# Where GpSimd splits the last four batches of keys, and the bias additions, in a gated two-layer kernel

## What is computed

```python
x = x + tanh(g_xattn[0]) * L0_xattn(ctx_1024, layernorm(x))   # dynamic time warping
x = x + tanh(g_ffn[0])   * L0_ffn(layernorm(x), w1, conv_w, conv_b, w2)
x = x + tanh(g_xattn[1]) * L1_xattn(layernorm(x), ctx_1024, ctx_1024, Wq, bq, ...)
x = x + tanh(g_ffn[1])   * L1_ffn(layernorm(x), input_patterns, ...)
```

```python
def bit_linear(x, w):
    return einsum('bsd,hd->bsh', act_quant(x), weight_quant(w))
h = bit_linear(x, w1)
h = silu(depthwise_conv1d(h, conv_w, conv_b))
return bit_linear(h, w2)
```

```python
q = (query @ Wq.T + bq) * 16 ** -0.5
k = key @ Wk.T + bk
v = value @ Wv.T + bv
return softmax(q @ k.T) @ v @ Wo.T + bo
```

## Time and profile before

| | us |
|---|---|
| median of 3 runs | 640.22 |
| lowest and highest | 637.81 and 644.44 |
| the profiled execution's own time | 635.6 |
| its span, first to last instruction | 633.9 |
| GpSimd busy | 110.0 (17%) |
| TensorE busy (matmuls) | 419.1 (66%) |
| VectorE busy | 444.8 (70%) |

### The profile page before, as it was taken

One profiled execution on the slowest core, in us unless ns is written; L12 is line 12 of the kernel. 1 busy time (PEld: TensorE's weight loads), 2 busy tenths in 40 slices (PEclk: granted clock), 3 DMA queues, 4 the chain that ended last, 5 costly groups with the idle time before them and its releaser, 6 DMA issues.

```text
span 633.9 us, 10214 instructions
## 1 busy us (share of the span) xinstructions
PE 419.1 (66%) x3424; PEld 298.9 (47%) x3424; DVE 444.8 (70%) x1714; ACT 272.3 (43%) x635; POOL 110.0 (17%) x238
## 2 busy tenths in 40 slices
PE   3897999523482403347899999999999655406306
PEld 3466776411262203234677777676455652106203
DVE  7546999899646796996778887875444574472573
ACT  3745444722303771004265555764433542451340
POOL 6770000000172560975000000000000000000000
PEclk9997899755595855578599999999999787755556
DMA  9600004392048830051025957900300360000002
GB/s 277 181 2 1 1 31 154 79 179 71 1 123 125 146 75 0 0 147 48 2 37 75 207 79 137 205 2 1 134 0 1 133 228 38 1 1 1 1 1 59
DMA packets 34665, 47.23 MB, mean 75 GB/s; under 512 B 5541, under 2 KB 32054, under 8 KB 32822
## 3 DMA queue, kind: packets, MB, share of 16 engines
q1 hardware_dynamic: 34614, 46.58, 31.0%
HBM read 37.87 MB, written 8.60 MB: 73 GB/s over the span
## 4 chain that ended last, share of the span: by engine, by line
PE 52%; DVE 28%; ACT 10%; issue 5%; POOL 4%; DVEq 0%; POOLq 0%; ACTq 0%
PE ps L1992 7%; PE ps L1922 4%; PE ps L1946 4%; DVE PR L1012 4%; ACT below L1626 4%; PE ps L1933 4%; PE ps L1768 3%; PE ps L1776 3%; PE ps L1908 3%; PE ps L1832 3%; PE ps L2118 2%; DVE prod L1008 2%; DVE hs L1108 2%; PE ps L1727 2%; DVE ct L1069 2%
## 5 line engine op out<-in xcount | busy, mean ns | idle before, releaser
L1173 DVE TENSOR_REDUCE negm<-ps 112x1 f32<-112x375 f32 x128 | 66.0, 544 | 11.8 <-PE ps L1922 8.7
L1597 ACT ACTIVATE E<-ps 125x448 f32<-125x448 f32 x96 | 52.0, 544 | 42.6 <-PE ps L1933 42.5
L1922 PE MATMUL ps<-ks,qs 96*112 96x375 bf16 x128 | 46.1, 376 | 3.7 <-ACT qs L1590 2.0
L2091 PE MATMUL ps<-cnt,same 128*128 128x3 bf16 (+4 forms) x40 | 6.9, 173 | 61.4 <-ACT below L1626 43.0
L1946 PE MATMUL ps<-E,v 125*32 125x112 f32 x768 | 42.1, 270 | 0.0
L1161 DVE TENSOR_REDUCE acts<-gel 128x4 f32<-128x448 f32 x32 | 19.8, 621 | 29.3 <-ACT gel L1560 29.3
L1933 PE MATMUL ps<-qs,ks 99*125 99x112 bf16 x384 | 39.9, 227 | 0.5 <-ACT E L1597 0.5
L1933 PEld LDWEIGHTS ps<-qs,ks 99*125 99x125 bf16 x384 | 34.7, 140 | 9.0 <-issue 6.0
L2091 PEld LDWEIGHTS ps<-cnt,same 128*128 128x128 bf16 (+1 forms) x40 | 4.4, 110 | 64.8 <-issue 64.8
L759 POOL CAST kp<-kx 128x750 bf16<-128x750 f32 x8 | 8.2, 1028 | 132.3 <-ACT path L1509 126.6
L1560 ACT ACTIVATE gel<-ps 128x448 f32<-128x448 f32 x32 | 17.3, 544 | 29.3 <-PE ps L1992 29.3
(11 more groups left out here) (371 smaller groups left out, 1164.0 us busy)
## 6 DMA issues: line engine op xcount, KB each, us to landing
ks<-key_parts SPq DMA_DIRECT2D x48, 187.5 KB, 6.6
piw<-fn_process_input_weights SPq DMA_DIRECT2D x8, 1024.0 KB, 4.9
key_parts<-kp SPq DMA_DIRECT2D x48, 93.8 KB
ctx_again<-in_ctx SPq DMA_DIRECT2D x7, 512.0 KB
keys<-kx SPq DMA_DIRECT2D x16, 187.5 KB, 2.1
kx<-keys SPq DMA_DIRECT2D x8, 375.0 KB, 6.4
ctxP<-in_ctx SPq DMA_DIRECT2D x8, 256.0 KB, 6.6
patn<-in_L_ffn_input_patterns SPq DMA_DIRECT2D x1, 2048.0 KB, 14.1
```

The costliest lines, as they stand in the source:

```text
L1173: drain(dve.tensor_reduce(negm[:, n:n + 1], bank(nm)[0:S, 0:SC], AX.X, ALU.max, negate=True), nm)
L1597: drain(fn(E[:, (KCH * f + c) % 6, :], bank(nm)[0:KC, 0:4 * S], ACT.Exp), nm)
L1922: fill(mm(bank(nm)[0:S, 0:SC], qs[0:SR, u // 4 % 3, n, :], ks[0:SR, u // 4 % 3, n, :], start=True, stop=True), nm)
```

## The change

The four splits of the last batches move from before the bias additions to behind them, and behind a new wait for all four counts of `q_split`, the end of VectorE's query split. The bias additions keep their own waits. No instruction is added or taken away but that wait.

```diff
             for c in range(HT - PT, HT):
                 pool.tensor_tensor(hs[:, c, :], hs[:, c, :], s2bc[:, :], ALU.mult).then_inc(scaled, 1)
 
-            for b in range(4, B):
-                split_keys(b)
-
             wait_drained(pool, "bo")
             pool.wait_ge(scaled, PT)
             pool.wait_ge(ln_ready, 3 * B)
             for b in range(B):
                 pool.tensor_tensor(x[:, b, :], x[:, b, :], gbo[:, :], ALU.add).then_inc(bias_added, 1)
+            pool.wait_ge(q_split, 4)
+            for b in range(4, B):
+                split_keys(b)
```

## The result

The changed kernel takes 633.29 us (median of 4 runs, 630.25 to 635.05) against 639.01 for the kernel before (4 runs, 636.85 to 644.44): a ratio of 0.9898, 95% interval 0.9854 to 0.9941. The forecast was 632.0 in a range of 627.5 to 638.0. The interval leaves out 1, so the gain is clear of noise, but it is small: it lies on the 1% at which the prediction parted "faster" from "within 1%". A second measurement, on another chip, gave 0.9908 (0.9874 to 0.9942). The profiled execution after took 630.25 us, its span 628.5 against 633.9.

The account below looks back on a forecast made before the run. The stage from 259.5 to 277.5 was taken as bound by VectorE, and VectorE by GpSimd. -6.7 - 2.7 + 0.4 + 0.4 + 0.4 = -8.2 us from 640.2 gave 632.0 us, range 627.5 to 638.0.

Parts of the forecast that it names:

- rival A: Rounding stage: TensorE's clock stays low, all of L1883 after 262.4 at 1.2 GHz; -5.4, 634.8 us; chance 0.16.
- rival B: Attention's start: GpSimd's splits slow, sync queue late, little instructions miss the gap; 634 us, up to 638; chance 0.10.
- Part 1: Rounding stage: with the splits gone VectorE is alone and L1883 ends at 270.8 against 277.5; -6.7 us.
- Part 2: Third layernorm and its transposes: 4.2 us instead of 6.94, -2.7; 0.4 put back for the clock in the projections.
- Part 3: Bias additions ahead of the splits: about one more query split instruction lies beside them; +0.4, between 0 and 1.2.
- Part 4: Splits beside the attention's start: maxima cost nothing, four little instructions on negm (L1220 to L1226) +0.4, between 0 and 6.2.
- the worst case of 6.2 us: Attention's start: each of the four little instructions waits for a whole subtraction, four times 1.56 us.
- Part 5: In-order sync queue: stores of batches 4 to 7 issued by 327.4, load_stack(3) not late by 1.5 us; cost 0.
- "I keep the clock of before": Attention's start: assumed TensorE's clock as in the kernel before, counting from 301.2; no term in the sum.
- rival C: Attention's start: splits stretch VectorE's maxima, with 1 us more on each; slower by net 15, 655 us; chance 0.07.
- rival D: Rounding stage: the change frees nothing, VectorE's long times would be its own; 640 us; chance 0.03.

Follow-up runs that it names:

- late splits: Changed kernel with the late splits waiting for the first neg_ready, about 11 us after the query split's end, instead of q_split: 645.30 us, ratio 1.0107.
- the two kernels without splits: The sixteen split instructions of batches 4 to 7 left out, in the changed kernel: 631.91 us, ratio 0.9902; in the kernel before: 631.81 us, ratio 0.9885.
- the one without the wait: Changed kernel without the new wait on q_split, so the splits follow the bias additions at once: 640.71 us, ratio 1.0026.
- PT = 0: VectorE makes all eight scalings, GpSimd none: changed kernel 623.08 and 623.07 us; kernel before 638.75 us; changed kernel with 30 filler matmuls behind L1883 624.04 us.
- fillers in the attention: Changed kernel with PT = 0 and matmuls that nobody reads ahead of score products in the attention's start: 622.79 us, ratio 0.9767.
- the one with fillers alone: Changed kernel with 30 matmuls that nobody reads behind L1883, ahead of the third layernorm's transposes: 627.67 us, ratio 0.9829.
- bias last: Changed kernel with the bias additions behind the late splits instead of ahead of them: 631.07 us, ratio 0.9875.

## Why the prediction was right, and by how much it was off

The time came within 1.3 us of the forecast, and some of that is luck: I counted from 640.22, and the kernel before measured 639.01 in the comparison. The gain was forecast at 8.2 us and measured at 5.7. The interval of the ratio (629.7 to 635.2 us from 639.01) also holds rival A's 634.8 and rival B's 634, so the time does not choose between them and the forecast; the rows of the stages do.

- **Part 1, the rounding stage.** Forecast -6.7, measured -5.9. VectorE's durations came as expected, but the scaling begun beside GpSimd's last one did not shorten: an instruction that has to wait for GpSimd's takes the whole wait, and I had let it make progress at a third of its speed. That is 0.5 us. TensorE's clock rose 4.8 us after the groups began to follow each other (264.05 to about 268.9), not 3.9: 0.3 more.
- **Part 2, the layernorm.** Forecast -2.7, measured -2.8. One reading in it was wrong: of the instructions up to 283.88 only the additions (L1119) read PSUM. The statistics read x from SBUF and kept their 0.42 us beside splits too, so the source alone is not what separates the instructions that GpSimd slows from the others. For the clock in the projections behind it I put back 0.4; it was 1.0, the upper bound.
- **Part 3, the bias additions.** Forecast +0.4, measured -0.7, the wrong sign: since the projections were late, the additions were over when the query split began, and the waits of the earlier trace rows vanished.
- **Part 4, the splits beside the attention.** Forecast 0 for the maxima and +0.4 for the little instructions; both 0. The maxima, out of PSUM, keep 0.55 us. The kernels with late splits and with late bias additions show that the little ones do wait when they miss the gap, 0.7 us growing to 2.9 and 2.3. The wait that I had allowed for is real, and so is the gap that spared them here. By the rows I gave 0.41 us for each, 1.6 for four; beside splits it was 2.2 for the four, and one cast alone waited 1.25 us. The Trainium skill ("SBUF — State Buffer", "SBUF: two separate sides") has the second to start wait for the whole instruction of the first, and that cast agrees: it ended with the subtraction. The total stays far below the worst case of 6.2 us, since the others met shorter rests of a split or none.
- **Part 5, the sync queue.** Forecast no cost, 1.5 us to spare; 3.2 were there, as the attention was slowed. The room beyond it was 3 us by my count and 1.0 by the landing of the sixth load (339.5, and L1922 starts at 340.50): I had taken the data for landed just after 337. It was not needed here. With the right landing rival B would have cost some 2 us more than I gave it.
- **What was not in the sum.** "I keep the clock of before" was the assumption that failed: +2.1 us in the attention's start, which takes 41.4 to 41.5 us in the six profiles in which the clock rose 16.7 to 17.6 us behind the query split, 42.0 where it rose 18.7 behind, and 43.6 in four with 22.6 to 22.7 (leaving out the two whose splits or additions lengthened it). Rival A had a low clock in the wrong place.

The sum by stages is -6.3 us against -8.2. That the late place is free and that the whole gain is the splits' absence from the rounding stage and the layernorm is shown by the two kernels without splits. Rival B needed slow splits, which did not occur; rival C, stretched maxima, is refuted by L1173's 0.55 us; rival D by L1112's. Left open is what sets the clock's rise in the attention's start. It came 16.7 to 18.7 us behind the end of the query split in seven profiles (the kernel before, the one without the wait, the four with PT = 0 but no fillers in the attention, the one with fillers alone) and 22.6 to 22.7 us in six (the changed kernel twice, bias last, late splits, and both without splits). So it is neither splits beside the attention nor scatter between executions; the kernel before with its splits left out rises late too. The fall ahead of it moved as well. In the kernel before the clock fell 0.5 us behind the end of the query split (0.86 granted from 301 to 302) and stayed low for 17.1 us; in the changed kernel it fell 2.2 us behind it (0.60 from 296 to 297) and stayed low for 20.5 us. All six late ones have the 2.2 and the 20.5. Of the other seven, six have a fall within 0.5 us of the query split's end and 17.1 us of low clock, and the kernel without the wait has 23.9. So 1.7 us of the 5.1 are a later fall, and 3.4 a longer stretch at the low clock, whose cause no run shows.

## What to carry to other kernels

In these runs GpSimd's casts and subtractions cost nothing beside VectorE instructions that read PSUM, nor beside the statistics. Beside a chain of products, subtractions, roundings and casts from SBUF to SBUF they cost most of their own duration (7 us for some 10 us of splits beside the query split). And an idle engine's help may be dearer than no help: three scalings given back to VectorE were worth more than the change itself. Before work is moved later, count through the in-order queue that carries its result: here 3.2 us were left over, and splits 11 us later stopped TensorE for 6.75 us. And price stretches of TensorE at both clocks: work that comes sooner may meet the low clock for longer.

## What the runs showed of the hardware that I had not expected

- TensorE was busy (by the modelled ends of its matmuls) in all of the 12 us from 304 to 316 and was still granted 0.50. In the changed kernel the high clock came 22.7 us behind the query split; with PT = 0 it came 17 us behind. Both kernels repeated their figure in a second profile.
- VectorE and GpSimd slow each other by turns to the instruction: a 0.39 us cast took 1.63 us beside a 1.56 us subtraction, and the subtraction 1.82. Beside VectorE's longer scalings (1.08 us) GpSimd's subtraction took 2.28.
- VectorE alone did sixteen instructions in 12.5 us, sooner than thirteen of them with GpSimd doing the other three (15.0).
- Of six loads issued within 2.6 us, each landed later behind its issue than the one before: 3.6 us for the first and 8.4 for the sixth in the kernel before. A first reader has to be counted from the sixth.
